# Products split into two tiles of 64 rows around the score matmuls, fixed banks, and a schedule in quarter slots, in a two-layer transformer kernel

## What is computed

```
for layer in (0, 1):                       # B = 32 samples, N = 256 tokens, C = 288, 16 heads of 18
    shift, scale, gate, shift2, scale2, gate2 = split(silu(c) @ W_mod + b_mod, 6)
    h   = layernorm(x) * (1 + scale) + shift
    q, k, v = heads(h @ W_qkv + b_qkv)     # layer 0 alone: q, k = layernorm over the 18 of a head, times gains
    att = softmax(q @ k.T * 18**-0.5) @ v
    x   = x + gate * (att @ W_proj + b_proj)
    h   = layernorm(x) * (1 + scale2) + shift2
    x   = x + gate2 * (gelu(h @ W1 + b1) @ W2 + b2)      # hidden width 1152
```

## Time and profile before

| what | value |
|---|---|
| median of 3 runs | 2551.22 us (2546.27 to 2555.2) |
| the profiled execution, span from first to last instruction | 2554.1 us |
| TensorE busy | 2371.3 us, 93% |
| TensorE weight loads | 1990.4 us, 78% |
| VectorE busy | 1852.2 us, 73% |
| ScalarE busy | 1626.7 us, 64% |
| GpSimd busy | 714.5 us, 28% |
| mean granted TensorE clock | 0.971 |
| chain that ended last | TensorE 63%, VectorE 11%, DMA 8%, issue 5%, SyncE's queue 5% |

### The profile page before, as it was taken

One profiled execution on the slowest core, in us unless ns is written; L12 is line 12 of the kernel. 1 busy time (PEld: TensorE's weight loads), 2 busy tenths in 40 slices (PEclk: granted clock), 3 DMA queues, 4 the chain that ended last, 5 costly groups with the idle time before them and its releaser, 6 DMA issues.

```text
span 2554.1 us, 56620 instructions
## 1 busy us (share of the span) xinstructions
PE 2371.3 (93%) x21219; PEld 1990.4 (78%) x21219; DVE 1852.2 (73%) x3456; ACT 1626.7 (64%) x3049; POOL 714.5 (28%) x938
## 2 busy tenths in 40 slices
PE   5558999999999999999999899999999999999998
PEld 3336878878888888888787788888888888888878
DVE  6357787787788777777677777777777777777764
ACT  3256666676666766767666666666676666666653
POOL 2012332332333233333222122223222222223222
PEclk8788999999999999999999999999999999999999
DMA  4776757756666666666846755566556655565531
GB/s 102 131 174 106 121 116 121 122 112 119 116 118 115 116 120 112 117 118 112 148 85 111 145 97 100 97 113 103 99 99 105 110 96 104 100 113 97 98 67 42
DMA packets 259208, 280.91 MB, mean 110 GB/s; under 512 B 25930, under 2 KB 243212, under 8 KB 258936
## 3 DMA queue, kind: packets, MB, share of 16 engines
q1 hardware_dynamic: 243888, 247.40, 55.8%
q10 hardware_dynamic: 15048, 29.89, 4.5%
HBM read 101.86 MB, written 26.73 MB: 50 GB/s over the span
## 4 chain that ended last, share of the span: by engine, by line
PE 63%; DVE 11%; DMA 8%; issue 5%; SPq 5%; ACT 4%; POOL 3%; DVEq 0%; POOLq 0%; ACTq 0%
PE psum L783 13%; PE psum L873 7%; PE psum_exp L783 7%; PE psum_max L783 7%; DMA attn_k_stack<-attn_qk_hi 5%; PE psum L933 5%; PE psum L935 5%; PE psum L934 5%; PE psum_exp L849 5%; DVE attn_maxima L1105 4%; PE psum_max L862 4%; SPq L1364 4%; DVE attn_qk_centred L1143 3%; PE psum L790 2%; ACT attn_probs L969 1%
## 5 line engine op out<-in xcount | busy, mean ns | idle before, releaser
L969 ACT ACTIVATE attn_probs<-psum_exp 128x1024 f32<-128x1024 f32 x512 | 526.9, 1029 | 391.4 <-PE psum_exp L849 377.6
L1105 DVE TENSOR_REDUCE attn_maxima<-psum_max 128x4 f32<-128x1024 f32 x512 | 620.6, 1212 | 83.0 <-PE psum_max L862 77.4
L1278 POOL TENSOR_TENSOR mlp_x<-mlp_x,mlp_gated 128x288 f32<-128x288 f32 x128 | 103.4, 808 | 1035.4 <-DVE mlp_gated L1122 1035.4
L783 PE MATMUL psum<-attn_ln_split,w_qkv_split 128*128 128x256 f32 (+3 forms) x2240 | 339.2, 297 | 5.1 <-DVE attn_neg_max_lo L1132 3.1
L933 PE MATMUL psum<-mlp_w_fc_hi,mlp_hidden_hi 128*128 128x288 f32 x1152 | 340.9, 296 | 2.9 <-DVE mlp_w_fc_lo L770 2.0
L934 PE MATMUL psum<-mlp_w_fc_lo,mlp_hidden_hi 128*128 128x288 f32 x1152 | 340.5, 296 | 0.0
L935 PE MATMUL psum<-mlp_w_fc_hi,mlp_hidden_lo 128*128 128x288 f32 x1152 | 340.2, 295 | 0.0
L783 PEld LDWEIGHTS psum<-attn_ln_split,w_qkv_split 128*128 128x128 f32 (+3 forms) x2240 | 284.2, 183 | 54.3 <-issue 25.8
L862 PE MATMUL psum_max<-attn_k_stack,attn_q_stack 62*128 62x256 f32 x2048 | 221.1, 294 | 103.6 <-DMA attn_k_stack<-attn_qk_hi 56.0
L873 PE MATMUL psum<-attn_probs,attn_v 128*32 128x256 f32 x4096 | 282.6, 394 | 1.1 <-ACT attn_probs L969 1.1
L849 PE MATMUL psum_exp<-attn_q_stack,attn_k_stack 64*128 64x256 f32 x2048 | 260.5, 332 | 20.9 <-ACT attn_probs L969 10.9
(11 more groups left out here) (170 smaller groups left out, 4222.1 us busy)
## 6 DMA issues: line engine op xcount, KB each, us to landing
attn_q_stack<-attn_qk_hi SPq DMA_DIRECT2D x256, 128.0 KB
attn_k_stack<-attn_qk_hi SPq DMA_DIRECT2D x256, 128.0 KB
attn_o_and_sums<-attn_o_transposed SPq DMA_DIRECT2D x256, 128.0 KB, 5.0
mlp_gate_and_gated_bias<-modulation ACTq DMA_DIRECT2D x64, 288.0 KB, 3.9
attn_qk_squares<-qk_rstd SPq DMA_DIRECT2D x32, 512.0 KB
attn_q_stack<-attn_qk_lo SPq DMA_DIRECT2D x128, 128.0 KB
attn_k_stack<-attn_qk_lo SPq DMA_DIRECT2D x128, 128.0 KB
attn_x<-in_x_dram SPq DMA_DIRECT2D x32, 288.0 KB, 7.6
```

Of the source, the lines that this page charges most:

```text
L783: mm = q.matmul(to, lhs, rhs, start=(i == 0), stop=(i == 6))
L969: q.activation(probs[r][:], ps_exp[:], ACT.Exp, scale=SCORE_SCALE).then_inc(S["exps"], 1)
L1105: q.tensor_reduce(maxes[g % 2][:, p // QUARTER, :, p % QUARTER, :], ps_max[:].rearrange("p a (t n) -> p a t n", t=TT), AX.X, ALU.max).then ...
L1278: q.tensor_tensor(xt, xt, gated2[:], ALU.add).then_inc(S["added2"], 1)
```

## The change

All offsets of the schedule are new and may lie at quarters of a slot (`STEP` = 4); some samples have offsets of their own (a third entry, a dictionary). The banks of every output are written out. `MAX` moves from the slot of `EXP` to half a slot behind it. Two outputs of 7 matmuls each (two chunks of q and k, the two token halves of v, of the projection, two chunks of fc1, the two token halves of fc2) are made together. Where a score product lies between the first and the second place of such a pair (`spaced`), every matmul is cut into one over rows 0 to 63 and one over rows 64 to 127: first the lower rows for the one output side by side with the upper rows for the other (`lower_and_upper`), then, behind a wait for these, the rows exchanged (`upper_and_lower`). Where no score product lies between, the pair is made with all rows. fc1 is always cut, for eight of its nine chunks. fc1 has one bank for each chunk, and the GELU nine instructions of 256 columns.

```diff
-XA_AT, STATS, RSTD, NORM, REST = (-60, -44), (-58, -42), (-56, -40), (-53, -39), (-51, -36)
-CHUNK_AT = {4: (-34, -26), 0: (-33, -23), 1: (-31, -22), 2: (-30, -20), 3: (-29, -18)}
-VALUE_AT = [(-25, -29), (-24, -17)]
-TAILS_AT = [(-17, -23), (-17, -17)]
-STACKS_AT = {0: (-16, -20), 1: (-15, -19), 2: (-15, -16), 3: (-14, -14)}
-MAX_AT, MAX_TR, NEG_AT, NEG_PLACE = -12, [(-5, -5), (3, 3)], [(-4, -4), (4, 4)], [(-3, -3), (5, 5)]
-EXP_AT, PV_AT = 0, 4
-O_MOVE, O_RECIP, O_NORM, O_HI, O_LO = (11, 12, 14, 18), (21, 21), (22, 22), (23, 24), (24, 25)
-XR_AT, GATE_AT, PROJ_AT = 26, 22, [27, 29]
-FC1_AT, FC2_AT, STORE_AT = 49, [(51, 51), (57, 61)], 68
+SPAN, STEP = 16, 4
+QK_PAIRS = [(0, 1), (2, 3)]
+LAST_CHUNK_AT = (-34.0, -26.5)
+QK_FIRST, QK_SECOND = [(-33.5, -26.0), (-32.25, -17)], [(-32.5, -25.5), (-32.25, -17)]
+V_FIRST, V_SECOND, V_OUT = (-25.25, -18.25, {1: -26.75}), (-25.25, -17.5), [(-25.5, -17.25), (-25.0, -17.0)]
+TAILS_AT = [(-19.0, -22.25), (-18.25, -17.25)]
+STACKS_AT = {0: (-16.0, -11.25, {0: -12.0, 1: -12.0}), 1: (-13.25, -14.5), 2: (-16.5, -12.0), 3: (-12.0, -12.0)}
+MAX_AT, MAX_OUT, MAX_TR, NEG_AT, NEG_PLACE = -11.5, -11, [(-4.0, -4.75), (5, 4.75)], [(-4.75, -4.0), (5.5, 4.5)], [(-3.0, -5.0), (5.5, 6.5)]
+EXP_AT, EXP_OUT, PV_AT, PV_OUT = 0, 0.25, 5.75, 5.75
+O_MOVE = [(13.75, 7.5), (17.25, 13.0), (17.75, 14.25, {ALL - 1: 13.75}), (18.5, 20.25, {1: 19.5, 2: 19.5})]
+XR_AT, GATE_AT, PROJ_FIRST, PROJ_SECOND = (24.25, 24.75), (15.5, 13.25), (27.75, 26.5), (28.0, 28.25)
+LAST_FC1_AT, FC1_AT, HIDDEN_AT, H_SPLIT = (49.75, 48.5), 49.75, 49.75, [(50, 50), (50, 50), (50, 50), (50, 50.25), (50, 50.5)]
+FC2_PARTS = [(0, 0, 14), (0, 14, 27), (1, 0, 14), (1, 14, 27)]
+FC2_AT = [(49.75, 50.25), (51.0, 51.5), (55.5, 52.25), (55.75, 54.75)]
+FC2_OUT, FC2_ADD, STORE_AT = [(56.5, 57.25), (59.25, 61.75)], [(57.0, 57.5), (60.75, 60.5)], (69.0, 63.5)
...
+FC1_FIRST, FC1_SECOND, LAST_FC1_BANK = (0, 1, 2, 3), ((5, 4, 0, 1), (6, 4, 0, 1)), (6, 6)
...
+def spaced(first, second):
+
+    between = [first + i / STEP for i in range(1, int(STEP * (second - first)) + 1)]
+    return any(pair_at(T, off) is not None for T in between for off in (MAX_AT, EXP_AT))
...
+        def lower_and_upper(q, low, high, half, split):
+
+            for i in range(len(WIDE_PAIRS) if split else 0):
+                done_low = part_matmul(q, low, i, LOWER, i == 0, False)
+                done_high = part_matmul(q, high, i, UPPER, i == 0, False)
+            if split:
+                done_low.then_inc(S[half], 1)
+                done_high.then_inc(S[half], 1)
+                halves[half] = halves.get(half, 0) + 2
+
+        def upper_and_lower(q, low, high, split):
+
+            for i in range(len(WIDE_PAIRS)):
+                first, last = not split and i == 0, i == len(WIDE_PAIRS) - 1
+                done_low = part_matmul(q, low, i, UPPER if split else ROWS, first, last)
+                done_high = part_matmul(q, high, i, LOWER if split else ROWS, first, last)
+            return done_low, done_high
...
+                if (g := due(T, FC1_AT)) is not None:
+                    for m in (0, 4):
+                        products = [fc1_product(g, m + i) for i in range(4)]
+                        bank_of(("fc1", g, m))
+                        bank_of(("fc1", g, m + 1))
+                        lower_and_upper(q, products[0], products[1], "fc1_half", True)
+                        bank_of(("fc1", g, m + 2))
+                        bank_of(("fc1", g, m + 3))
+                        lower_and_upper(q, products[2], products[3], "fc1_half", True)
+                        for i, pair in enumerate((products[0:2], products[2:4])):
+                            q.wait_ge(S["fc1_half"], CHUNKS // 2 * 2 * g + m + 2 * i + 2)
+                            low, high = upper_and_lower(q, *pair, True)
+                            low.then_inc(S["fc1"], 1)
+                            high.then_inc(S["fc1"], 1)
...
-                        q.activation(hidden[use % 2][:, 0:n, :], psum[banks["fc1", g, j][0]][:, 0:n * N].rearrange("p (c n) -> p c n", n=N),
-                                     ACT.Gelu_apprx_tanh).then_inc(S["gelu"], 1)
+                        for i, m in enumerate(group):
+                            q.wait_ge(S["fc1"], CHUNKS * g + FC1_ORDER.index(m) + 1)
+                            q.activation(hidden[use % 2][:, i, :], psum[banks["fc1", g, m][0]][:, 0:N], ACT.Gelu_apprx_tanh).then_inc(S["gelu"], 1)
```

More of the change, by code:

```diff
@@ L164, in use, with use_pair @@
         table[key] = (on[0], before)
[L166 to L174, removed]
+    def use_pair(keys, pair):
+        for key, bank in zip(keys, pair):
+            use(key, bank)
     for T in SLOTS:
-        for n, at in enumerate(MOD_AT[4:]):
+        for n, at in enumerate(MOD_AT):
             if T == at:
-                take(("mod", n), T, T + .9)
-        if T == MOD_TR[1]:
-            take(("mod_turn", 0), T, T + 1.9)
+                use(("mod", n - 4), (2 if n < 4 else 5) + n % 2)
+        if T in MOD_TR:
+            part = MOD_TR.index(T)
+            use(("mod_turn", part), (0, 6)[part])
         if (s := pair_at(T, EXP_AT)) is not None:
@@ L199, in bank_table @@
[L199 to L202, removed]
-            if (g := due(T, VALUE_AT[t])) is not None:
-                take(("v", g, t), T, T + 1.9)
-            if (g := due(T, FC2_AT[t])) is not None:
-                take(("fc2", g, t), T, T + 1.6)
+            use(("var", g), VAR_BANK)
         for n in range(2):
             if (g := due(T, MAX_TR[n])) is not None:
-                take(("turn", g, n), T, T + 1.6)
+                use(("turn", g, n), TURN_BANKS[n][g // B])
@@ L213, in bank_table @@
-            take(("fc1", g, FC1_USES - 1), T, T + 1)
+            for m, bank in enumerate(FC1_FIRST + FC1_SECOND[g // B]):
+                use(("fc1", g, m), bank)
+        if (g := due(T, FC2_AT[0])) is not None:
+            use_pair([("fc2", g, t) for t in range(TT)], FC2_BANKS[g // B])
     return table
@@ L943, in slots_pe @@
+                if (g := due(T, LAST_FC1_AT)) is not None:
                     q.wait_ge(S["hi2"], g + 1)
@@ new lines, in slots_pe @@
+                    wide_matmul(q, bank[:, 0:N], w1, slice(8 * P, 9 * P), acts2, slice(0, N), True).then_inc(S["fc1"], 1)
+                for pair, first, second in zip(QK_PAIRS, QK_FIRST, QK_SECOND):
+                    if (g := due(T, first)) is not None:
+                        bank_of(("qk", g, pair[0]))
+                        bank_of(("qk", g, pair[1]))
+                        lower_and_upper(q, *[qk_product(g, c) for c in pair], "qk_half", spaced(T, when(second, g)))
+                    if (g := due(T, second)) is not None:
+                        split = spaced(when(first, g), T)
+                        if split:
+                            q.wait_ge(S["qk_half"], halves["qk_half"])
+                        low, high = upper_and_lower(q, *[qk_product(g, c) for c in pair], split)
+                        low.then_inc(S["qk_mm"], 1)
+                        high.then_inc(S["qk_mm"], 1)
@@ new lines, in slots_pe @@
+                if (g := due(T, PROJ_SECOND)) is not None:
+                    split = spaced(when(PROJ_FIRST, g), T)
+                    if split:
+                        q.wait_ge(S["proj_half"], halves["proj_half"])
+                    low, high = upper_and_lower(q, *[proj_product(g, t) for t in range(TT)], split)
+                    low.then_inc(S["proj"], 1)
+                    high.then_inc(S["proj"], 1)
+                if (g := due(T, FC1_AT)) is not None:
[12 more added lines that the diff above has]
+                            high.then_inc(S["fc1"], 1)
@@ L1032, in slots_act @@
                 for t in range(TT):
-                    if (g := due(T, after(VALUE_AT[t], 1))) is not None:
+                    if (g := due(T, V_OUT[t])) is not None:
                         q.wait_ge(S["v_mm"], TT * g + t + 1)
```

287 lines of the change are left out of this document (173 added, 114 removed).

## The result

The changed kernel takes 2818.55 us (median of four runs, 2812.8 to 2822.16) against 2552.13 us (2546.27 to 2555.2): the ratio is 1.1048, 95% interval 1.1031 to 1.1065. I had forecast 2620, with 2690 as the upper end.

A forecast was written before the change was run, and what follows sets the result against it. TensorE's order sets the pace, with layer 0's transfer chain late next: layer 0 +3.0 us on 30 samples (+90), layer 1 -0.75 on 28 (-21), 2554.1 + 69 = 2623, median 2620 us; own range 2560 to 2690, 8-in-10 range 2460 to 2690.

The forecast's parts named there:

- three moves and the gate at 2.8 us in the chain: Layer 0, SyncE's queue: three `O_MOVE` and the gate's load lengthen the transfer chain from 21.25 to 24.05 us.
- lower bound of 2.3 (issues): Layer 0 chain: the added transfers cost at least their issue times on SyncE, 3 x 0.61 + 0.5 = 2.3 us.
- upper of 3.9 (bytes): Layer 0 chain: the added transfers cost at most their 528 KB at 137 GB/s, 3.9 us.
- (a): Rival, chance 0.27: the idle half of the DMA window takes up layer 0's moves; faster, 2481 us.
- (b): Rival, chance 0.08: the chain also gets shorter than before and all is TensorE's; 2450 us.
- (c): Rival, chance 0.08: the two layers cancel, layer 0's chain growing by 1.5 us with the clock staying; 2552 us.
- (d): Rival, chance 0.07: a pair of half-height matmuls takes 0.135 us instead of 0.12, some 80 us more; 2700 us.
- 20.5: Layer 1, first stretch: transfer chain of 20.5 us against TensorE's 19.6, costing 0.9 us a sample.
- 1.0 us of 0 to 1.8: Layer 0, behind TensorE's stand: the granted clock falls, costing 1.0 us a sample, range 0 to 1.8.
- 15.6: Layer 0, second stretch (`MAX` of pair 0 to `EXP` of pair 7): TensorE's work, 16.40 - 0.6 - 0.2 us.
- changes of tile: TensorE's switches of row count or columns, about 0.2 us each: fewer save some 0.6 us a sample in layer 0, 1.5 in layer 1.
- 14.8: Layer 1, second stretch on TensorE: 17.58 - 1.85 (fc2 quarter moved) - 1.0 (switches) + 0.2 - 0.1 us.

The follow-up runs named there:

- e8_before_moves: Kernel before, with layer 0's o moves 0 to 2 and the gate's load put between tails and first stack on SyncE's queue: 2711.16 us, ratio 1.0617.
- e11_issues: Kernel before, plus three 1 KB transfers a sample on SyncE's queue between tails and first stack in layer 0: 2654.39 us, ratio 1.0421.
- e12_bytes: Kernel before, plus three 129 KB transfers a sample on ScalarE's queue in the same stretch of layer 0: 2584.95 us, ratio 1.0135.
- e4_whole: Changed kernel with all products made whole, as single matmuls with all rows instead of 64-row pairs: 2957 us.
- e5_fill16: Changed kernel with 16 unused identity matmuls before TensorE's wait for the stack at pair 0, layer 0: 2779.82 us.
- e6_fill16_y: Changed kernel with the 16 filling matmuls, and VectorE's `QK_Y` of chunk 4 moved behind the reduce of pair 3's maxima: 2743.38 us.
- e9_l1: Changed kernel, layer 0's moves and gate out of the chain, `QK_Y` later; layer 1's banks, maxima transpose and first v half moved: 2612.1 us, ratio 1.0211.

## Why the prediction was wrong

**What bounds the kernel, and the transfers: right in layer 0.** The step that no row of before showed directly, three moves and the gate at 2.8 us in the chain, came out at 24.20 against 24.05. The stacks land 2.9 us later than before, and 3.5 later in e8_before_moves: between the lower bound of 2.3 (issues) and the upper of 3.9 (bytes). To lean to the issues was right, as e11_issues (0.7 us of stretch for each) and e12_bytes (0.9 for 387 KB) show; the bound itself was too low. Rivals (a) and (b), the idle half of the window, fell with e8_before_moves, and so did (c), which had the chain 1.5 longer and the clock free. Rival (d), dear pairs, fell with the fc1 rows of e4_whole. In layer 1 the agreement, 20.54 against 20.5, is in part luck: TensorE waits for the stacks only 0.33 us a sample where 0.9 was forecast, and its own order fills the rest.

**The clock: right mechanism, too small.** It falls once a sample, as said. I took 1.0 us of 0 to 1.8; 5.7 us of low clock in the stretch are worth 2.6 by the rows of e11_issues. The 1.4 of e5_fill16 is what is left of that when VectorE's wait comes out from under it.

**The second stretch of layer 0: wrong.** It was put at 15.6 and 1.0 for the clock, and is 19.69, 3.1 more. By what stands in the changed kernel itself: 1.6 are the clock (2.6 for 1.0), 0.6 the wait for the maxima, 0.9 TensorE's own work (16.5 for 15.6: 16.97 less 0.46 of waits in e6_fill16_y). By removal, one after the other, VectorE's wait counts 1.35 and the clock's excess 0.4; the rest, 1.4, is then the same 0.9 and `EXP`'s wait of 0.5 for ScalarE's exponentials.

The 0.9 were lost in the sum. It took 0.6 off this stretch for changes of tile, but the number of rows changes ten times in it, before and after. And 32-column outputs are left four times (three before), now mostly for score products, which the count "to the full array" left out; such a step takes as long. In e6_fill16_y the last four products with v and the next `EXP` start

```profile
644.90 0.40 PE L964 MATMUL psum<-attn_probs,attn_v 128*32 128x256 f32 x4
645.23 0.50 PE L937 MATMUL psum_exp<-attn_q_stack,attn_k_stack 64*128 64x256 f32 x4
```

0.33 us apart, as in the earlier trace rows the step from there to all rows. The second maxima transpose was taken off the first stretch (0.25) and not put on this one, which has both. The kernel before without its 0.21 us of waits and with that transpose gives 16.33 - 0.21 + 0.25 = 16.4, the 16.5 nearly. Within it one thing is open: the norm's transposes and the projection each start 0.4 us behind the last matmuls of a `MAX`, where the earlier trace rows have 0.2 and layer 1 of the same kernel has 0.2 and 0.1.

The steps that failed: "15.6", which takes 0.6 of savings from tile changes that the measured work does not show and puts every wait at nothing, and the 1.0 for the clock. I had listed the change of `QK_Y` in the diff and not asked what it waits for and what is queued behind it.

**The second stretch of layer 1: wrong, by waits.** 14.8 was put against 17.57. The waits in it are, as means over samples 39 to 60, 1.5 us (bank 4 behind the norm), 0.55 (v for bank 4, behind `PV`), 0.4 (maxima) and 0.25 (q and k for bank 4), 2.7 us; 17.57 - 2.7 = 14.8. In e9_l1 the same account gives 14.0 with 0.9 us of work moved out. So TensorE's own work came out at the forecast number, in part by luck: the forecast took 1.0 for changes of tile, and there are two fewer changes of rows in this stretch (8 for 10) and as many exits from 32 columns as before (three), while 0.4 us of waits for maxima that stood in the 17.58 of before are counted apart here. The step that failed is the banks: four uses of one bank next to each other. The new bank table gives fixed banks, and I had taken banks at nothing without laying the uses of bank 4 in the order of TensorE.

**The sum.** The two second stretches are worth 3.1 x 30 + 2.8 x 28 = 171 us; with the 24 us of start, turn and end and 2620 this is 2815. The range was too narrow upward: its bound for the clock, 1.8, was under the price that the runs show, and it had none for TensorE's own work and for waits that the new order brings.

**ScalarE's nine GELU:** no wait for them is among TensorE's.

## What to carry to other kernels

A transfer put into a queue ahead of the last one that somebody waits for can cost its turn however small it is, 0.7 us here for 1 KB; look for what a moved transfer overtakes and for what it makes wait. When a forecast takes TensorE's own work from durations, go once through the new order with every wait of every engine that feeds it: what is queued behind that wait, and who wrote the bank last. A wait or a slow stretch removed alone gives less than its length where a second one lies under it: remove them one after the other before adding up, and look for samples in which only one of them occurs, as those of e11_issues with and without the low clock.

## What the runs showed that I had not expected

A slow clock hid a wait: 12.5 us for the maxima in the changed kernel, 30.0 when the stand was filled. So the time of this stretch at full clock could not be had by scaling. And 16 small matmuls that nobody needs, put in a stand of 4 us, made the kernel faster by 39 us (2818.55 to 2779.82), with the transfers where they were.
